# Top-25 neighbour search of the gathered tile: one long search replaced by 16 short ones and a search among their 128 winners

## The reference, cut to what matters

```
mask   = A != 0                                   # (8, 1024, 1024)
scores = where(mask, -arange(1024), -inf)
vals, idx = top_k(scores, 25)                     # the 25 neighbours of lowest index
feats  = x[idx], or -inf where there are fewer    # (8, 1024, 25, 128)
agg    = feats.max(axis=2)                        # and 0 in the max where degree <= 25
out    = relu(concat([x, agg]) @ W + b)
result = layernorm(x + out)
```

## Time and profile before

| | |
|---|---|
| median of three runs | 584.74 us |
| profiled execution | 587.01 us, of which the span from first to last instruction is 585.3 us |
| TensorE busy | 509.4 us (87%) |
| VectorE busy | 530.7 us (91%) |
| ScalarE busy | 400.4 us (68%) |
| GpSimd busy | 289.2 us (49%) |
| mean granted TensorE clock | 0.95 of 2.4 GHz |

### The profile page before, as it was taken

The page is one execution under the profiler, slowest core; times in us unless marked ns, Lnnn a source line. Parts: engine busy times, 40 slices in busy tenths (PEclk is TensorE's granted clock), DMA queues, the critical chain, the costliest instruction groups (busy, mean ns, idle before and its releaser), DMA issues.

```text
span 585.3 us, 13962 instructions
## 1 busy us (share of the span) xinstructions
PE 509.4 (87%) x4600; PEld 346.0 (59%) x4600; DVE 530.7 (91%) x977; ACT 400.4 (68%) x761; POOL 289.2 (49%) x462
## 2 busy tenths in 40 slices
PE   3687998899969998899988999799988999779982
PEld 2444675567645675566755576556755667546761
DVE  5976999999998999999998988999999999998894
ACT  6832667468974788658965788568886589546744
POOL 3633573357434774247533565237742475337700
PEclk9587999999999999999988999799999999999997
DMA  7753544466655645565535645267565653021102
GB/s 259 188 160 83 138 126 102 123 137 134 97 112 146 168 111 124 136 155 125 136 93 148 141 130 111 78 171 170 110 120 140 157 123 61 2 60 44 47 8 73
DMA packets 84418, 69.48 MB, mean 119 GB/s; under 512 B 56259, under 2 KB 72902, under 8 KB 84294
## 3 DMA queue, kind: packets, MB, share of 16 engines
q1 hardware_dynamic: 77894, 54.93, 38.9%
q0 software_dynamic: 6400, 13.12, 8.5%
HBM read 50.99 MB, written 4.19 MB: 94 GB/s over the span
## 4 chain that ended last, share of the span: by engine, by line
PE 38%; DVE 34%; issue 12%; DVEq 7%; ACT 4%; DMA 3%; POOL 0%; POOLq 0%; SPq 0%; ACTq 0%
PE pair L1074 30%; DVE part L801 15%; DVE hot L796 5%; DVE g_feat L874 4%; DVEq L871 2%; DVE g_val L842 2%; PE misc L1119 2%; DVE agg_t L901 2%; DVEq L940 2%; PE p_V L1057 1%; DMA adj_sb<-in_adj 1%; PE misc L1120 1%; DVE g_score L844 1%; DVEq L1008 1%; DVEq L917 1%
## 5 line engine op out<-in xcount | busy, mean ns | idle before, releaser
L1074 PE MATMUL pair<-hot,x_part 128*128 128x128 bf16 (+3 forms) x3120 | 411.9, 280 | 32.9 <-DVE part L801 28.2
L1074 PEld LDWEIGHTS pair<-hot,x_part 128*128 128x128 bf16 x3120 | 239.0, 99 | 141.5 <-issue 46.3
L801 DVE TENSOR_REDUCE part<-pair 128x128 f32<-128x1024 f32 (+1 forms) x256 | 279.3, 1100 | 25.5 <-PE pair L1074 24.0
L485 POOL DMA_INDIRECT g_feat<-in_x,g_idx x200 | 193.7, 968 | 127.0 <-issue 81.3
L605 ACT ACTIVATE V<-p_V 128x512 bf16<-128x512 f32 x98 | 57.7, 588 | 68.9 <-PE p_V L1057 68.9
L532 POOL TENSOR_TENSOR y_sb<-relu_sb,x_sb 128x128 f32<-128x128 f32 x64 | 30.6, 479 | 149.1 <-ACT relu_sb L659 148.5
L633 ACT ACTIVATE hot<-V,first_bias 128x1024 bf16<-128x1024 bf16 x56 | 64.0, 1142 | 25.6 <-PE pair L1074 25.6
L796 DVE TENSOR_SCALAR hot<-V 128x1024 bf16<-128x1024 bf16 x224 | 79.4, 375 | 0.0
L648 ACT ACTIVATE hot<-distance,one 128x1024 bf16<-128x1024 bf16 x56 | 63.9, 1141 | 0.2
L641 ACT ACTIVATE distance<-V,second_bias 128x1024 bf16<-128x1024 bf16 x56 | 63.6, 1136 | 0.0
L598 ACT ACTIVATE mask<-adj_sb 128x1024 bf16<-128x1024 uint32 x56 | 58.7, 1049 | 6.5 <-DMA adj_sb<-in_adj 6.5
(11 more groups left out here) (92 smaller groups left out, 431.9 us busy)
## 6 DMA issues: line engine op xcount, KB each, us to landing
adj_sb<-in_adj SPq DMA_DIRECT2D x56, 512.0 KB
g_adj<-in_adj SPq DMA_DIRECT2D x8, 512.0 KB, 4.4
x_sb<-in_x SPq DMA_DIRECT2D x8, 512.0 KB, 4.6
out<-y_sb SPq DMA_DIRECT2D x7, 512.0 KB, 5.2
g_feat<-in_x,g_idx POOLq DMA_INDIRECT x200
maskT<-mask SPq DMA_TRANSPOSE x49
out<-y_sb SPq DMA_DIRECT2D x1, 448.0 KB
w_sb<-in_W SPq DMA_DIRECT2D x1, 128.0 KB, 6.2
```

What stands on the lines that cost most here:

```text
L485: pool.indirect_dma_start(out=g_feat[w][:, k, :], out_offset=None, in_=x_rows, in_offset=bass.IndirectOffsetOnAxis(ap=g_idx[w][:, k:k + 1] ...
L801: dve.tensor_reduce(part[:, par(q, s), :, p], slots_of(q, s, p).rearrange("f k i -> f i k"), AX.X, ALU.max).then_inc(s_used, 1)
L1074: last = pe.matmul(dst, x_part[:, q, part_no, kb], one_hot, start=(first and part_no == 0), stop=(final and part_no == PARTS - 1))
```

## The change

The search for tile 0 is made in another way, and part of it moves to other engines.

- Columns are dealt to 16 classes, column j to class j mod 16, by a strided view. `g_score` is now stored class by class.
- The scores of batches 1 to 7 are made by two engines: `find0` on ScalarE (the sign of `g_adj`, read in class order, at the end of its stage 1) and `score0` on GpSimd (a product with `falling`, 128 x 1024 float32, at the head of its stage 2, before the gathers of that stage).
- VectorE finds the 8 largest of each class: 16 searches of 64 elements (two steps of 8). Then it finds the 32 largest of the 128 candidates: four `MAX8` and three `MATCH_REPLACE8` of 128 elements, and one short reduction.
- A row could lose a neighbour if one class held more than 8 of its first 25. A row whose largest eighth value of a class is above its 26th value is flagged in `viol`; a flag sets the level of stage 7 to 2, and then tile 7 and tile 0 are both done again by the full search.
- The row numbers and bounds are made on GpSimd (`index0`, seven short instructions at the end of its stage 7) in place of VectorE.
- TensorE's sum of violations in stage 1 waits for the flag too, and the linear layer of tile 0 moves behind the read of the level in stage 7.
- For batch 0 the scores and the row numbers are still made on VectorE.

```diff
+            def score0(batch):
+                wait(s_found, batch)
+                pool.tensor_tensor(g_score[0][:, :], g_score[0][:, :], falling[:, :], ALU.mult).then_inc(s_score, 1)
+            def index0(batch, bp):
+                val, pick, step = g_val[0], g_pick[0], 3 * (batch - 1)
+                wait(s_ex, SEARCH * (batch + 1))
+                pool.tensor_scalar(first0[:, :], val[:, 0:1], 0.0, val[:, 0:1], ALU.is_equal, ALU.add).then_inc(s_index, 1)
+                pool.wait_ge(s_index, step + 1)
+                pool.tensor_scalar(pick[:, :], val[:, 0:K], 0.0, first0[:, :], ALU.is_equal, ALU.mult).then_inc(s_index, 1)
...
                 for s in range(1, NT):
+                    if s == 2 and not last:
+                        score0(2 * i + q + 1)
                     if s <= 5:
                         gather0(i, q, s)
...
                     redo(i, q, s)
+                    if s == MT and not last:
+                        index0(2 * i + q + 1, nq)
...
+            def find0(batch):
+                act.wait_ge(s_adj0, 16 * (batch + 1))
+                act.wait_ge(s_ex, SEARCH * batch)
+                nc.scalar.activation(by_class(g_score[0]), columns_by_class(g_adj[0].bitcast(U32)), ACT.Sign).then_inc(s_found, 1)
...
+                if st <= SCANS:
+                    each = CLASSES // SCANS
+                    scores_of = by_class(g_score[0])
+                    for c in range(each * (st - 1), each * st):
+                        ins = dve.max(found[:, c], scores_of[:, c])
+                else:
+                    r, replace = divmod(st - SCANS - 1, 2)
+                    candidates = found.rearrange("p c r -> p (c r)")
+                    val = g_val[0][:, RANKS8 * r:RANKS8 * (r + 1)]
+                    if replace:
+                        ins = dve.match_replace(candidates, val, candidates, 0.0)
                     else:
+                        if r == 0:
+                            dve.tensor_reduce(eighth[:, :], found[:, :, RANKS8 - 1], AX.X, ALU.max)
+                        ins = dve.max(val, candidates)
...
-            EXTRACT = {1: {4: 0}, 2: {1: 1, 4: 2}, 3: {3: 3}, 4: {3: 4}, 5: {1: 5, 3: 6}, 6: {}, 7: {1: 7, 3: 8}}
+            EXTRACT = {1: {}, 2: {4: 1}, 3: {1: 2, 3: 3}, 4: {1: 4, 3: 5}, 5: {1: 6, 2: 7, 3: 8}, 6: {}, 7: {1: 9}}
...
             def violations(i, q):
                 pe.wait_ge(s_viol, 2 * i + q + 1)
+                pe.wait_ge(s_missed, 2 * i + q + 1)
```

More of the change, by code:

```diff
@@ L301, in build, with redo_no, by_class, columns_by_class @@
         ON_VECTOR = (4, 5, 6, 7)
+        def redo_no(i, q, s):
+            return NT * (2 * i + q) + s - 1
+        def by_class(row):
+            return row.rearrange("p (c k) -> p c k", c=CLASSES)
+        def columns_by_class(row):
+            return row.rearrange("p (k c) -> p c k", c=CLASSES)
         def pair_no(i, q, s, p):
@@ new lines, in remake @@
+            def remake(i, q, s, n):
+                pool.dma_start(g_adj[1][:, :], adj_tiles[bass.ds(2 * NT * i + NT * q + s, 1)]
+                               .rearrange("a p n -> p (a n)")).then_inc(s_fdma, 16)
+                before = pool.snap(redone, min_val=0, max_val=(MAIN + B) * 16 * (K + 1))
+                pool.wait_ge(s_fdma, before + 16)
+                pool.sem_inc(s_fadj, 1)
+                wait(s_fidx, n + 1)
+                if s == 0:
+                    wait(s_fagg, n)
+                gather(1, s_fdma, range(K))
+                pool.wait_ge(s_fdma, before + 16 * (K + 1))
+                pool.reg_add(redone, redone, 16 * (K + 1))
+                pool.sem_inc(s_fg, 1)
@@ L697, in step @@
                         copy_V(*to_rank, 1)
+                    if s == 1 and not last:
+                        find0(2 * i + q + 1)
                     if s in (6, 7) and not is_first(i, q):
@@ new lines, in extra_reduce, with scores, indices @@
+                dve.tensor_tensor(maxima, maxima, more[:, :, :], ALU.max).then_inc(s_xdone, 2 if s == MT else 1)
+            def scores(w):
+                return dve.scalar_tensor_tensor(out=by_class(g_score[w]), in0=columns_by_class(g_adj[w]), scalar=0.0,
+                                                in1=by_class(falling), op0=ALU.not_equal, op1=ALU.mult)
+            def indices(w, batch, bp, signal):
+                val, pick = g_val[w], g_pick[w]
+                dve.scalar_tensor_tensor(out=pick[:, :], in0=val[:, 0:K], scalar=0.0,
+                                         in1=val[:, 0:1].to_broadcast([P, K]),
+                                         op0=ALU.is_equal, op1=ALU.mult)
+                dve.tensor_scalar(g_bound[w][:, bp, 0:1], val[:, K:K + 1], 0.0, -BIG, ALU.is_gt, ALU.mult)
+                dve.tensor_scalar(g_bound[w][:, bp, 1:2], val[:, 0:1], 0.0, None, ALU.is_gt)
+                dve.drain()
+                dve.scalar_tensor_tensor(out=pick[:, :], in0=pick[:, :], scalar=1.0, in1=val[:, 0:K],
+                                         op0=ALU.max, op1=ALU.max)
+                dve.drain()
+                dve.scalar_tensor_tensor(out=g_idx[w][:, :], in0=pick[:, :], scalar=-1.0,
+                                         in1=row_base[:, bass.ds(batch, 1)].to_broadcast([P, K]),
+                                         op0=ALU.mult, op1=ALU.add).then_inc(signal, 1)
@@ L867, in gathered_max, with search_again @@
+            def search_again(batch):
+                scores(1)
+                for r in range(ROUNDS):
+                    val = g_val[1][:, RANKS8 * r:RANKS8 * (r + 1)]
+                    dve.drain()
+                    dve.max(val, g_score[1][:, :])
+                    dve.drain()
+                    if r < ROUNDS - 1:
+                        dve.match_replace(g_score[1][:, :], val, g_score[1][:, :], 0.0)
+                indices(1, batch, 0, s_fidx)
             def gathered_max(w, bp, signal, steps):
@@ L971, in step @@
                         if (s, p) in GATHERED:
+                            if (s, p) == (7, 0) and not begin:
+                                dve.wait_ge(s_bound, 2 * (2 * i + q))
                             if GATHERED[s, p][0] == 0:
@@ L1027, in copy_turned @@
                                 ).then_inc(s_tcopy[1], 1)
-            for st in range(3):
-                first_step(st)
+            scores(0).then_inc(s_score, 1)
+            for st in range(1, SCANS + 2):
+                search(0, st)
             for t in range(1, MT + 1):
```

168 lines of the change are left out of this document (77 added, 91 removed).

## The result

The changed kernel takes 576.83 us (median of four, 574.64 to 580.86) against 585.36 of before on the same chips (583.03 to 588.83). The ratio is 0.9846, with an interval of 0.9812 to 0.988: faster by 8.5 us (1.5%), where 12.7 were forecast. The profiled execution took 576.68 us, span 574.9, at a mean granted clock of 0.975.

A forecast was written before the change was run, and what follows sets the result against it. VectorE and TensorE were nearly full in turn, with GpSimd's gathers binding L to F; seven batches at 1.85 + 0.2 us gave 14.4, less 2 for the clock: 587.0 became 574.6 profiled, 572 us median, range 566 to 580.

The forecast's parts named there:

- L to F: From the linear layer after TensorE's wait for levels (L) to the first reduction of gathered rows (F): 38.3 to 38.1 us.
- VectorE's own path: Stages 2 to 5: the time from L to F without late gathers, put at 36.2 us.
- F to L: Stages 6, 7 and 1, from the first reduction of gathered rows to the next L: 28.52 us, to shrink by 1.85.
- the gain of 0.2: Stages 2 to 5: late gathers behind `score0` let L to F shrink by only 0.2 us per batch.
- the landing: Before F: time from the last gather's end until its data has landed and signalled, taken at 3.3 us.
- the forecast range (1 to 3): At F: VectorE idle 1 to 3 us in most batches, ended by the gather's DMA, as a sign of being right.
- VectorE's 1.9 us of idle time before F: Before F: VectorE stands idle some 1.9 us, from which slowed one-hots could be paid.
- the case that `score0` itself is slowed: Stage 2: if the product takes 3.1 us, gathers land 0.9 later, 6 us of gain are lost: 578 us.
- the wait of 1.26 us: Stage 4: GpSimd's wait of 1.26 us swallows the gathers' delay and is gone after the change.
- The clock: Growing TensorE idle time in stage 6 lowers the clock: 2 us on the run, 1.35 us in one or two batches.
- The rival "TensorE sets stages 7 and 1": Stages 7 and 1: TensorE sets the pace once VectorE is lighter, so no change, 585 us; chance 0.12.
- Hidden parts: `find0` on ScalarE (about 1.05 us), `index0` on GpSimd, the flag and the `g_adj` load: all costed at nothing.

The follow-up runs named there:

- the fastest version: Changed kernel with scores back on VectorE, 7, 5, 4, 5, 4 gathers in stages 1 to 5, and PSUM buffers in strict turn: 559.70 us, ratio 0.9553.

## Why the prediction was right, and where it was off

**What binds L to F: right.** GpSimd does. Three edits that take the product away, shorten it or put the gathers ahead of it bring L to F to 36.5 to 36.9 each in batches 2, 3 and 6, near the 36.2 taken for VectorE's own path. Only the third removes the waits in all batches. DMA waits at F came in batches 0, 1, 3, 4 and 6; in 2 and 5 there is none, because stage 4 was long there from the held one-hot.

**F to L: right.** The term was 1.85 us per batch. With the buffers in turn on both sides, F to L is 26.6 to 26.9 in batches 1 to 3 and 5 against 28.4 to 28.7, 1.8 us. In the changed kernel it was 1.6 on average (11.2 / 7), but between 0.4 and 2.3 in single batches. The doubled buffer took 1.3 to 1.4 back in batches 1, 3 and 5, a term that the prediction didn't have. In batches 1 and 3 this doesn't show, because the kernel before had lost 1.6 to 1.8 at the same place, with its clock low; in batch 5 it had lost nothing, and the gain is 0.4. In batch 4 stages 6 and 7 lost clock, and the gain is 0.8. Of the terms in it, the row numbers were too small: 0.75 in the queue and up to 0.2 behind them, where the run with them on VectorE shows 1.2.

**L to F, the gain of 0.2: mis-sized.** `score0` was taken at 2.2 us and took 2.45, and the gathers of stage 2 moved 1.7 to 2.4 us, 2.0 on average, and not 1.8. GpSimd was done at 35.5, not 34.8. What saved it was the landing, and that was luck: in batches 3 and 6, where F waits, F came 1.96 and 2.06 us after the last gather, where 3.3 was taken from two distances of before; in batch 1 it took 3.76, and L to F got 0.9 us longer than before. The five waits lay between 0.51 and 2.65 us; only those of batches 1 and 4 are in the forecast range (1 to 3). Batch 4 is its own case: GpSimd's gap of 4.36 us lies ahead of the gathers, and there is no slack left to hide it.

**What contention costs: the step that was too small.** The prediction let one-hots beside GpSimd be paid from VectorE's 1.9 us of idle time before F, and priced only the case that `score0` itself is slowed. In stage 2 that held in batches 1, 3 and 6; in 2, 4 and 5 the stage is 0.2 to 0.5 us longer than before, although VectorE has less to do there. GpSimd cost more in two other places: in batch 0, where eight one-hots stand on TensorE's path (held 1.65 us, and up to 2.8 with what followed), and in stage 4, where the wait of 1.26 us went, as forecast, so that the eight subtractions of `split_rest` now start together with a one-hot (1.2 us of L to F in batches 2 and 5; in batch 4, where it falls into stage 5, the late gathers cover it). One-hots of 1024 elements rose from

```profile
L796 DVE TENSOR_SCALAR hot<-V 128x1024 bf16<-128x1024 bf16 x120 | 52.9, 452 | 0.0
```

to 549 ns. The Trainium skill, SBUF, State Buffer, section Who interferes with whom, says that the engine that gets the pair first holds it for the whole instruction and the other is blocked. In batch 0 the trace agrees: the product lasts from 45.17 to 47.51, the first one-hot from 45.23 to 47.56. In stage 4 it doesn't: the one-hot waited through a run of instructions, 3.19 us, and not through one; the measurement decides.

**The clock: the loss didn't come.** 2 us were put on the run for it. In the profiled pair the mean granted clock rose from 0.95 to 0.975; between F of batch 0 and F of batch 7 the changed kernel lost some only in batch 4, behind its late gathers, and the kernel before in batches 1 to 5. But this pair is not typical: 28 other executions of the kernel before, taken beside the experiments, have 0.926 to 0.979, half of them 0.967 or more, and the four of the changed kernel 0.962 to 0.975. So a loss is not shown, and a gain isn't either. The price of 1.35 us itself, read from stage 1 of batch 4, is that of a low clock just behind a doubled buffer: with the buffers in turn that stage took 11.55 us, at full clock.

The sum of the span is then: 14.4 us forecast without the clock, less 1.8 from F to L, 1.1 from L to F and 1.1 in batch 0, is 10.4, as in the profiled pair. The term for the clock, which was not needed, covered half of what the others lacked. That the time fell into the range owes something to this and to the short landings.

**The rival "TensorE sets stages 7 and 1"** rested on its 9.18 us busy of 9.69. Stage 7 took 7.5 us all the same, with 63 matmul records in place of 75: TensorE works ahead of VectorE's stage borders, and what it does within them is not a fixed amount of work. In stage 2 it does set the pace: there the fastest version has it busy for 9.22 of 9.22 us.

**Hidden parts.** `find0` took 1.95 us and `index0` seven short instructions, and neither is seen on the path: the residual that waits for `relu` starts 1.3 us after L in both kernels. `index0` on GpSimd is the part of the move that pays, 8.7 us against VectorE in the fastest version. Moving the scores is the part that costs: without it the change was worth 16 us (0.9715) and not 8.5.

**Open:** what GpSimd's queue does in the gap of batch 4, which stands in the kernels with and without the change, and why the gathers of batch 1 land late.

## What to carry to other kernels

When work moves to an engine that is "half idle", ask what stands behind it in that engine's queue and who waits for that, before counting what the first engine saves: here the move of the scores took 1.2 us (1.9 in class order) off VectorE and put 2 us ahead of 20 gathers that had 0.8 us of slack by the prediction's estimate. Short instructions at the end of a stage that VectorE paces are worth moving; a long one at the head of a queue with a due time is not, unless what is due goes first. And look for coincidences with a period: a buffer count that doesn't divide the number of groups, and two engines whose instructions start together so that one holds the other up, cost 1 to 3 us in some batches only, and each became visible when the batches were compared one by one.

## What was unexpected of the hardware

- Reads with a step of 64 bytes (every 16th element of 4 bytes): 1946 ns for 1024 elements on ScalarE against 1049 for the mask of the same size without a step (which is written as bf16 and not float32), 1882 to 1899 on VectorE against 1210, and 252 against 207 for a search of 64. The Trainium skill, SBUF, State Buffer, section Specifications (TRN2), gives 16-byte lines with a penalty for each new one; the trace agrees in direction, and the penalty here is 0.65 to 0.9 ns per element.
- A one-hot of 128 elements on VectorE lasted 3.19 us when it began 0.01 us after GpSimd's residual, which a run of eight subtractions followed without a gap; one that began 0.33 us into such a run took 0.18. The one of batch 4 began 0.06 us before the residual and still lasted 3.49, so the order of the starts doesn't explain it. What decides is open.
- From the end of the last gather's instruction to F, where F waited, took 1.7 to 3.8 us in the five such batches of the changed kernel, so one such distance is no price for a landing.
